# A lead of its own for each kind of step in the planned order of a four-layer graph kernel

## What is computed

```python
h = jnp.maximum(_layernorm(x, axis=-1), 0.0)
x = x + _L0_gnn_ref(h, adj, W, b)
...
x = x + _L1_gnn_ref(h, adj, W, a_src, a_dst)
...
x = x + _L2_gnn_ref(h, adj, Wq, bq, Wk, bk, Wv, bv, Wo, bo)
...
x = x + _L3_gnn_ref(h, adj, W_heads, a_heads, W_out, a_out, w1, b1, w2, b2, ln_gamma, ln_beta)
```

## Time and profile before

| | |
|---|---|
| median of 3 runs | 1876.4 us (1875.9 to 1878.53) |
| the profiled execution | 1877.61 us, span 1875.7 us |
| TensorE busy | 1746.8 us, 93% |
| TensorE weight loads busy | 1661.5 us, 89% |
| VectorE busy | 1573.2 us, 84% |
| ScalarE busy | 1539.7 us, 82% |
| GpSimd busy | 862.1 us, 46% |
| granted TensorE clock, mean | 0.980 |

### The profile page before, as it was taken

One profiled execution on the slowest core, in us unless ns is written; L12 is line 12 of the kernel. 1 busy time (PEld: TensorE's weight loads), 2 busy tenths in 40 slices (PEclk: granted clock), 3 DMA queues, 4 the chain that ended last, 5 costly groups with the idle time before them and its releaser, 6 DMA issues. The chain is left out here.

```text
span 1875.7 us, 45892 instructions
## 1 busy us (share of the span) xinstructions
PE 1746.8 (93%) x15880; PEld 1661.5 (89%) x15880; DVE 1573.2 (84%) x5359; ACT 1539.7 (82%) x3634; POOL 862.1 (46%) x1492
## 2 busy tenths in 40 slices
PE   0789999999999999999999999999999999999985
PEld 0678999999999999999999999999999999999874
DVE  6478988888889888888998888889888889988863
ACT  2368988888899888888988888898888889888872
POOL 4224544445554444555444445544444554443442
PEclk8799999999999999999999999999999999999997
DMA  5000000000000000000000000000000000000000
GB/s 165 12 24 2 20 23 19 24 25 24 13 24 19 19 24 24 24 13 24 19 23 19 24 24 21 16 19 24 18 24 24 13 24 19 24 13 19 18 18 12
DMA packets 31206, 43.83 MB, mean 23 GB/s; under 512 B 3328, under 2 KB 26880, under 8 KB 30976
## 3 DMA queue, kind: packets, MB, share of 16 engines
q1 hardware_dynamic: 30976, 40.91, 6.7%
HBM read 32.38 MB, written 8.52 MB: 22 GB/s over the span
## 5 line engine op out<-in xcount | busy, mean ns | idle before, releaser
L775 POOL TENSOR_TENSOR cx<-cx,rden 128x64 f32<-128x64 f32 x256 | 78.3, 327 | 511.8 <-DVE cx L1426 511.8
L919 ACT ACTIVATE pb<-lg,hmin 128x256 f32<-128x256 f32 x512 | 227.1, 499 | 42.3 <-DVE hmin L1408 39.8
L966 PE MATMUL ps<-wout,hid 128*128 128x256 f32 x1536 | 228.7, 290 | 1.8 <-ACT hid L933 1.0
L927 ACT ACTIVATE pT<-ps 128x512 f16<-128x512 f32 x256 | 145.5, 590 | 97.9 <-PE ps L1177 92.7
L1408 DVE CUSTOM_DVE_ANT_0 lg<-ps,maskp 128x256 f32<-128x256 f32 x512 | 190.9, 419 | 26.9 <-PE ps L1160 24.7
L966 PE MATMUL ps<-wh,hT 128*128 128x256 f32 x1536 | 212.4, 288 | 0.8 <-DVE whs L1324 0.8
L966 PE MATMUL ps<-pT,whs 128*128 128x256 f32 x1536 | 206.0, 283 | 3.0 <-DVE pT L1373 1.9
L966 PEld LDWEIGHTS ps<-wout,hid 128*128 128x128 f32 x1536 | 196.3, 190 | 9.9 <-ACT hid L933 1.4
L765 POOL TENSOR_TENSOR hid<-fu,hid 128x512 fp32r<-128x512 f32 x128 | 166.7, 1303 | 76.8 <-ACT hid L933 76.8
L966 PEld LDWEIGHTS ps<-pT,whs 128*128 128x128 f32 x1536 | 192.4, 191 | 4.2 <-DVE pT L1373 2.5
L966 PEld LDWEIGHTS ps<-wh,hT 128*128 128x128 f32 x1536 | 191.2, 190 | 3.9 <-DVE whs L1324 1.3
(11 more groups left out here) (188 smaller groups left out, 4790.0 us busy)
## 6 DMA issues: line engine op xcount, KB each, us to landing
tbc<-t_dram SPq DMA_DIRECT2D x32, 512.0 KB, 3.7
xin<-x_in SPq DMA_DIRECT2D x32, 256.0 KB, 2.7
out<-xs SPq DMA_DIRECT2D x32, 256.0 KB, 2.2
t_dram<-st_rows SPq DMA_DIRECT2D x128, 1.0 KB
xs<-a_heads SPq DMA_DIRECT2D x4, 128.0 KB, 5.5
pT<-a_heads SPq DMA_DIRECT2D x4, 128.0 KB, 4.5
lg<-W_out SPq DMA_DIRECT2D x2, 256.0 KB, 5.2
tb<-adj SPq DMA_DIRECT2D x1, 256.0 KB, 2.8
```

What stands on the lines that cost most here:

```text
L919: last = act.activation(pb[h % 2][:, c, :], lg[h % 2][:, c, :], ACT.Exp, bias=hmin[h % 2][:, c:c + 1], scale=-1.0)
L927: act.activation(pT16[h % 2][:, 0], bank(head_bank(h)), ACT.Copy).then_inc(pT16_hi, 1)
L966: last = pe.matmul(dst, lhs(a, t), rhs(b, t), start=(not low and opens and n == 1), stop=(low is not False and closes and n == terms * len ...
```

## The change

A table `OWN_LEAD` gives most kinds of step a number, by name and for all batches and heads, and `arrange()` adds it to `rest` beside the stage's `LEAD`. A `..._hi_part` has the number of its product; a kind that isn't in the table has 0. Numbers go from +118 (`pT16_lo`) to -99 (`hid_hi`). `LEAD` itself, the costs, the predecessors and every emitted instruction are the same. In the changed file all lines behind the first ones stand seven lines further down.

```diff
             for st in todo:
-                st["rest"] += LEAD[section(*st["step"][:2])]
+                st["rest"] += LEAD[section(*st["step"][:2])] + OWN_LEAD.get(st["step"][0].removesuffix("_hi_part"), 0)
...
+        OWN_LEAD = dict(pT16_lo=118, elu=100, wo=72, peak=64, st_rows=42, q=23, scores=21, s_cols=18, top=17,
...
+                        k_lo=-12, x_deg=-12, wh_hi=-30, exps=-32, elu_exp=-35, rows=-81, leaky=-88, hid_hi=-99)
```

More of the change, by code:

```diff
@@ L582, in adj_preln_kernel @@
         GRAIN, LEAD = 0.2, (34.0, 34.0, 33.0, 33.0)
+        OWN_LEAD = dict(pT16_lo=118, elu=100, wo=72, peak=64, st_rows=42, q=23, scores=21, s_cols=18, top=17,
+                        probs_T=15, v=15, amj=13, out_b2=12, scale=10, st_out=10, p_T=9, attend=8, mj_lo=8, y=8,
+                        f1_hi=7, inv_std=7, v_a=7, x_bo=6, elu_relu=4, f1_lo=4, ffn1=4, k=4, x_beta=4, y_gamma=4,
+                        cols=3, pT16_hi=3, q_hi=3, x3=3, aggr=2, mj=2, rows_lo=2, mi=1, rows_hi=1, spread=1, tmin=1,
+                        wh_lo=1, x1=1, mj_hi=-1, probs_lo=-1, s_exp=-1, x_mi=-1, final=-2, stats=-2, x2=-2, f1_full=-3,
+                        k_hi=-3, store=-3, v_r=-3, load=-4, q_lo=-5, wh=-6, t_spread=-7, v_c=-7, ffn2=-8, v_b=-8,
+                        k_lo=-12, x_deg=-12, wh_hi=-30, exps=-32, elu_exp=-35, rows=-81, leaky=-88, hid_hi=-99)
         ISSUE = (0.07, 0.04, 0.05, 0.05, 0.05)
```

## The result

The changed kernel takes 1848.72 us (median of 4 runs, 1847.7 to 1849.05); the kernel before, on the same chip, 1877.47 (1875.9 to 1881.05, 4 runs). The ratio is 0.9833, 95% interval 0.9814 to 0.9852: 28.8 us or 1.7% less, where 20.8 us were forecast; the interval leaves 1 out. The profiled execution took 1847.7 us, span 1846.0, mean granted clock 0.982.

The account below looks back on a forecast made before the run. TensorE was taken as the bound, measured by weight loads. Gains 0.82 + 0.38 less costs 0.42 and 0.2 gave 0.58 us a regular batch, 20.8 in all with irregular ones: 1856 us; forecast 1843 to 1870, range 1836 to 1888.

Parts of the forecast that it names:

- What bounds the kernel: TensorE: its weight loads, busy 51.30 of 54.30 us a batch, measure the headroom, 3.0 us, rather than its matmuls, 0.7.
- the rest of the 3 us: TensorE's idle weight loading beyond the 1.68 us of named waits a batch: claimed to be issue, which no order removes.
- `values` 4 and the last `scores`: TensorE waits for `pT16_lo`: a head weight product in front covers both, gain 0.53 + 0.29 = 0.82 us a batch.
- `ffn2`: TensorE's wait for `f1_hi` on ScalarE: `rows` 2 and a `leaky` now come behind `f1_hi`, gain 0.38 us a batch.
- ScalarE's queue before `wo`: ScalarE's chain from `probs_hi` 0 to the `rows_hi` that `wo` needs comes late: cost 0.42 us, bounds 0 and 0.9.
- the 0.48 for two `wh_hi`: On ScalarE two `wh_hi` instead of one stand before `probs_hi` 0: 0.48 us more in front of `wo`.
- its bound of 0: No cost before `wo`, if ScalarE reaches `probs_hi` 0 earlier.
- GpSimd's queue before `rows` 1: Four `hid_lo`, norm steps and others follow each other on GpSimd, so `rows` 1 comes late: cost 0.2 us, bounds 0 to 1.5.
- My 19.1 against 18.8 us: Chain through GpSimd to the end of `rows` 1, 19.1 us, against TensorE's work meanwhile, 18.8: `rows` 1 0.3 us late.
- the rival that was to turn the sign of the whole change: GpSimd becomes the bound: batch 54.87 us, total 1887 us; slower, mostly by GpSimd's chain or ScalarE's, had 0.25.
- The irregular batches: Batches outside 6 to 20 become regular: 0.22 us a batch, from the mean 54.47 to 54.25, over 26 batches.
- The variant with half of the two costs: The sum with all named waits vanishing, but half the costs on ScalarE before `wo` and GpSimd before `rows` 1: 1848 us.

Follow-up runs that it names:

- experiment 10: Changed kernel with `x3` directly behind `tmin` 4, `top` 4 behind `rows_lo` 0 and `peak` 4 behind `stats` 3: 1834.23 us, ratio 0.9758 to the kernel before.
- experiment 2: Kernel before, in 12 regular batches `wh` 1 moved to right behind `p_T` 5 and `cols` 1 moved on VectorE: 1896.46 us (before 1877.96).
- experiment 1: Kernel before, in 13 regular batches `leaky` of head 3 moved from between `f1_full` and `f1_hi` to behind `f1_hi`: 1877.39 us (before 1877.96).
- experiment 6: Changed kernel's timeline, then that kernel with `inv_sum` 1 in front of `tmin` 2: 1857.42 us; with `peak` 2 also behind `top` 2: 1852.43 us.
- experiment 7: Changed kernel's timeline around the long `tmin`, then that kernel with `tmin` 3 moved in front of `x3`: 1847.76 us, ratio 0.9829 to the kernel before.

## Why the prediction was right, and where not

The sign, the place and the kind of the gain were right; 1848.7 us lies in the range and in the interval of the forecast (1843 to 1870), 7 us below the 1856 that the sum gave. By its own steps:

- **What bounds the kernel.** TensorE's waits are the time, and weight loads measure them: a batch fell by 0.84 us with 51.15 us of loads in it. The matmul share would have allowed 18 us (26 x 0.7); 28.8 were measured, 27.4 of them in the 26 batches, and 44 to 46 in experiment 10. The row of the loads was the right one, and with it the Trainium skill's rule (Perfetto Trace Analysis, "Identifying the Most-Contended Engine"). That the rest of the 3 us is issue which no order removes was too strong: 0.3 us of the fall lies outside the named waits.
- **`values` 4 and the last `scores`, 0.82.** 0.54 + 0.20 = 0.74 us of waits went; `scores` keeps 0.11. No run shows this gain by itself. The reason as I put it, a product moved in front covers the wait, is by itself a loss: experiment 2 made that move, with `values` 4 left in front of the spread, and was 18.5 us slower. What I called one term is a package over four queues, of which `leaky` 0 behind `scale` 5, `inv_sum` 5 in front of `tmin` 0, `probs_hi` 5 in front of `s_exp` 6, `probs_lo` 5 in front of `tmin` 1 and `wh` 3 in front of `attend` 5 are candidates by the two orders. The changed kernel has them all and the waits are gone; I hadn't looked for them, so that this term came out is in part luck.
- **`ffn2`, 0.38.** Gone, and experiment 1 shows it by itself: 0.25 of it is kept in the batch.
- **ScalarE's queue before `wo`, -0.42.** This term was mis-sized. `wo` starts 6.54 us behind `probs_T` 0 (787.46 to 794.00 in experiment 6), and 0.35 of that is the wait of `probs_T` 1 in between; without it 6.19, where 6.92 - 0.71 = 6.21 was forecast. ScalarE needs 6.27 to the end of `rows_hi` 3 (the first half of the row at 793.14), where 6.33 + 0.48 + 0.02 - 0.2 = 6.63 was forecast. So the margin is -0.08 and not -0.42. The part that failed is the 0.48 for two `wh_hi` in front of `probs_hi` 0: ScalarE was through with both in time, and `probs_hi` 0 starts 0.74 us behind `probs_T` 0 (788.20), where the kernel before has 0.82. The forecast had named this case, as its bound of 0. No line for `wo` behind `rows_hi` came up in the waits, which was to show it. A cost of nearly the forecast size is paid, one step earlier, since `probs_T` 1 waits for `scale` 1, over VectorE and GpSimd, two queues that this term had left out.
- **GpSimd's queue before `rows` 1, -0.2.** The chain is as tight as I had it, but not late. The timeline shows that the norm step behind `hid_lo` 4 finds GpSimd just finished:

```profile
769.21 1.29 POOL L772 TENSOR_TENSOR hid<-fu,hid 128x512 fp32r<-128x512 f32 x1
770.66 0.23 POOL L729 TENSOR_SCALAR ve<-mv 128x2 f32<-128x2 f32 x1 [0.16 <-DVE mv L1259]
```

  0.16 us of idling, where the earlier trace rows have 2.71. The transposes of `rows` 1 don't wait, and `st_rows` waits 0.1 us less than before. My 19.1 against 18.8 us is 19.56 against 19.70 in the timeline (value product from 753.85, end of `rows` 1 at 773.41, its transposes at 773.55): both sides were put too short, TensorE's by more, and the sign is the other one. This is the rival that was to turn the sign of the whole change; it missed by 0.14 us.
- **What I left out, -0.38.** `q` (0.15) and `probs_T` 2 (0.23) wait, and experiment 10 shows why: the order lays `f1_lo` beside `tmin` 4. I had priced every instruction by a row of a regular batch of the kernel before, in which the two never met; `tmin` had 428 ns there and has 527 now.
- **The irregular batches, 0.22 a batch.** As forecast: all are alike, 5.7 us. Filling gave 2.4 us, of the size by which it varies between runs of one order, though the changed order's are the shorter ones; I can't assign them. Draining gave nothing.

In sum +0.82 +0.38 -0.42 -0.2 = 0.58 was forecast for the regular batch and 0.84 measured. Both costs were put at places where they didn't fall, and the costs that did fall (`probs_T` 1 0.35, `probs_T` 2 0.23, `q` 0.15) come to 0.73. That the forecast was near is partly the luck that 0.62 and 0.73 are alike, against some 0.3 us of small gains that I hadn't counted. The variant with half of the two costs, 1848, is what was measured, but not for its reason.

## What to carry to other kernels

In a kernel with three queues over 80% busy a move in one queue has partners in the others: before a step is moved, follow what its results release on every engine, and see which steps stand in those queues behind the released ones. Single moves of a good order can each cost time that the whole order wins. And when a new order makes a group's mean duration longer (here 428 to 527 ns with the same instructions), look for what now runs beside it; that one row led to half as much again as the change itself had given.

## What the runs showed of the hardware

A VectorE instruction with two inputs in SBUF doesn't run beside a GpSimd TENSOR_TENSOR that has two: the later one waits until the other ends, whatever its size. Measured: `tmin` 1.51 us instead of 0.42, `top` on 128x2 elements 1.21 instead of 0.15, `peak` 0.47 instead of 0.18; and in the other direction `f1_lo` 1.46 instead of 1.30, where half a `tmin` had begun 0.12 us before it. VectorE instructions with one input in PSUM keep their 0.68 us beside it. This is what the Trainium skill says in the page SBUF — State Buffer, sections "SBUF: two separate sides" and "Who interferes with whom": a VectorE instruction with two SBUF inputs contends with a GpSimd instruction that reads SBUF, and whichever starts first holds the shared port pair to its end. The rows above agree with it.

They agree for a GpSimd instruction with one tile too. `scale` is a TENSOR_SCALAR of two instructions, usually 0.48 us each. In the changed kernel the first one of `scale` 2, here 0.65 us long, has run for 0.34 us when `top` 4 starts (746.75 and 747.09 in the rows of experiment 7), and `top` 4 takes 0.31 us instead of 0.15: both end at 747.40. The other way round `tmin` comes first, in experiment 6:

```profile
849.90 0.42 DVE L1355 CUSTOM_DVE_ANT_0 tb<-tbc,mask3p 128x256 f32<-128x256 f32 x1
850.03 0.90 POOL L757 TENSOR_SCALAR ea<-ea,rs 128x256 f32<-128x256 f32 x1 [1.13 <-DVE rs L1376]
...
850.25 0.42 DVE L1355 CUSTOM_DVE_ANT_0 tb<-tbc,mask3p 128x256 f32<-128x256 f32 x1
```

Both halves of `tmin` 2 keep their 0.42 us, and the first half of `scale` 1 takes 0.90. One thing the rows leave open. Here the GpSimd instruction waited for both halves, and so does `scale` 2 beside `tmin` 3 in the kernel before (0.85 us instead of 0.48). But `f1_lo`, which begins as soon behind a first half (745.19 and 745.31), gets in between the two and makes the second one wait, and so does `normal` 2 beside `tmin` 2 in the kernel before (0.51 us instead of 0.42). The first two are TENSOR_SCALAR, the others TENSOR_TENSOR; that this makes the difference isn't shown.
